# Attention visits of a slot brought together behind the gate, in a fused FFN-attention-FFN block on one core

## The reference, cut to what matters

```
x = x + 0.5 * ffn(layernorm(x))
x = x + attn(layernorm(x))        # 16 heads of 16, 4 KV heads, rope, softmax over 1024 keys
x = x + 0.5 * ffn(layernorm(x))

ffn:  top-8 of 32 experts, cut where the renormalised sum passes 0.8, inner width 96
      out += (silu(x @ Wg.T) * (x @ Wu.T)) @ Wd.T * combine[:, e]     for each expert e
attn: softmax(q @ k.T / 4) @ v, then @ Wo.T
```

## Time and profile before

| what | us |
|---|---|
| median of three runs (2396.12 to 2398.11) | 2397.57 |
| the profiled execution | 2396.93 |
| its span, first to last instruction | 2395.1 |
| TensorE busy | 2280.0 |
| VectorE busy | 1568.7 |
| ScalarE busy | 1235.5 |
| GpSimd busy | 1052.1 |

### The profile page before, as it was taken

One profiled execution on the slowest core, in us unless ns is written; L12 is line 12 of the kernel. 1 busy time (PEld: TensorE's weight loads), 2 busy tenths in 40 slices (PEclk: granted clock), 3 DMA queues, 4 the chain that ended last, 5 costly groups with the idle time before them and its releaser, 6 DMA issues.

```text
span 2395.1 us, 48463 instructions
## 1 busy us (share of the span) xinstructions
PE 2280.0 (95%) x19616; PEld 1517.8 (63%) x19616; DVE 1568.7 (65%) x3106; ACT 1235.5 (52%) x1966; POOL 1052.1 (44%) x864
## 2 busy tenths in 40 slices
PE   0399998999999999999999999999999999999999
PEld 0388885556555555555555555565555655688887
DVE  3855657977777777777777776776776763345443
ACT  1333332256655656656566656666666656633332
POOL 0366664443443443344344433433433433466665
PEclk9999999999999999999999999999999999999999
DMA  4201112101010110111011011100110010010010
GB/s 193 72 19 37 27 41 55 38 18 43 16 35 24 31 38 20 31 26 41 15 33 41 14 34 29 31 19 24 31 30 22 13 29 19 11 37 29 19 38 19
DMA packets 96343, 80.24 MB, mean 33 GB/s; under 512 B 40308, under 2 KB 88692, under 8 KB 95736
## 3 DMA queue, kind: packets, MB, share of 16 engines
q1 hardware_dynamic: 95256, 76.09, 11.3%
q10 hardware_dynamic: 864, 1.05, 0.1%
HBM read 64.25 MB, written 12.85 MB: 32 GB/s over the span
## 4 chain that ended last, share of the span: by engine, by line
PE 91%; DVE 5%; DMA 1%; ACT 1%; issue 1%; SPq 0%; POOL 0%; ACTq 0%; POOLq 0%; DVEq 0%
PE PS L1069 42%; PE PS L1087 21%; PE PS L1099 11%; PE PS L1130 11%; PE PS L1041 2%; DMA arena<-wo 1%; DVE arena L859 1%; PE PS L1111 1%; PE PS L1016 1%; PE PS L1044 1%; PE PS L1171 1%; PE PS L1157 1%; PE PS L1025 0%; DVE arena L836 0%; DVE amax L700 0%
## 5 line engine op out<-in xcount | busy, mean ns | idle before, releaser
L1069 PE MATMUL PS<-XT,WGU 128*128 128x256 f16 x9216 | 1117.3, 274 | 51.2 <-DVE WGU L711 31.7
L1069 PEld LDWEIGHTS PS<-XT,WGU 128*128 128x128 f16 x9216 | 875.2, 98 | 282.7 <-issue 132.6
L520 POOL TENSOR_TENSOR arena<-arena 128x512 f16<-128x512 f32 x384 | 446.8, 1163 | 1198.6 <-ACT arena L596 1198.6
L859 DVE TENSOR_REDUCE arena<-PS 128x1 f32<-128x512 f32 x1024 | 658.2, 685 | 370.6 <-PE PS L1099 368.7
L619 ACT ACTIVATE arena<-PS,fac 128x512 f32<-128x512 f32 x1024 | 646.4, 684 | 236.3 <-PE PS L1111 235.0
L589 ACT ACTIVATE arena<-PS,fac 128x512 f32<-128x512 f32 x384 | 263.9, 687 | 762.1 <-PE PS L1069 762.1
L1087 PE MATMUL PS<-WD,arena 128*128 128x256 f16 x4608 | 568.0, 273 | 1.8 <-POOL arena L520 1.6
L1087 PEld LDWEIGHTS PS<-WD,arena 128*128 128x128 f16 x4608 | 432.4, 98 | 141.3 <-issue 89.8
L515 POOL TENSOR_TENSOR arena<-arena 128x512 f32<-128x512 f32 x384 | 492.0, 1281 | 50.2 <-DVE arena L844 49.0
L836 DVE SCALAR_TENSOR_TENSOR arena<-arena,PS 128x512 f32<-128x512 f32 x384 | 261.2, 680 | 284.1 <-ACT arena L589 283.7
L1099 PE MATMUL PS<-arena 48*128 48x512 f16 x1024 | 312.3, 382 | 7.3 <-DMA arena<-k_scratch 4.6
(11 more groups left out here) (114 smaller groups left out, 856.0 us busy)
## 6 DMA issues: line engine op xcount, KB each, us to landing
arena<-ce_scratch SPq DMA_DIRECT2D x256, 128.0 KB, 3.3
arena<-wgu SPq DMA_DIRECT2D x2, 3072.0 KB, 17.5
arena<-q_scratch SPq DMA_DIRECT2D x96, 64.0 KB, 2.2
arena<-ktab_c SPq DMA_DIRECT2D x16, 256.0 KB, 4.1
q_scratch<-arena SPq DMA_DIRECT2D x32, 128.0 KB, 1.7
out<-X SPq DMA_DIRECT2D x8, 512.0 KB, 3.0
X<-wd SPq DMA_DIRECT2D x1, 3072.0 KB, 28.1
X<-x SPq DMA_DIRECT2D x1, 3072.0 KB, 15.5
```

The lines of the kernel that those rows point to most:

```text
L520: pool.tensor_tensor(hs[1][:, d % HS, :], tw[d % 2], hs[0][:, d % HS, :], ALU.subtract).then_inc(lo_done, 1)
L859: dve.tensor_reduce(mx[:, half * REP * QT + c:half * REP * QT + c + 1], PS[:, B_MAX + half, :], AX_X, ALU.max).then_inc(max_taken, 1)
L1069: ins = pe.matmul(PS[:, b, j * HALF_G:(j + 1) * HALF_G], WGU[w][:, kt, part * CHUNKS + c + j, :], XT[r][:, k % 2, kt, half * HALF_G:(half ...
```

## The change

The visits are arranged anew. TensorE runs visits 0 and 1 directly behind the gate, then up and down, then a second event, then visits 2 and 3, then the first event. VectorE takes both visits' maxima before `gated` and `product`. ScalarE takes visit 0's exponentials before the tanh of the gate, and visit 1's where they were. The table gives four visits to each lead-in slot (ten slots instead of thirteen and a third), and afterwards two, with four in every tenth slot. As the counts are even now, visit 0 is always an even one (scores alone) and visit 1 an odd one, which begins with the value matmuls. Nothing is added or removed: 514 visits with v >= 0, 40 before them, 384 slots. Visits now end in slot 307 instead of 310, and some events move by a few slots.

```diff
-        for pos in range(3 if v < 0 or (d - FIRST) % 5 == 4 else 2):
+        for pos in range(4 if v < 0 or (d - FIRST) % 10 == 9 else 2):
...
 # ScalarE
+                if (d, 0) in VISIT:
+                    visit(VISIT[d, 0])
                 if d + 1 < SLOTS:
                     gate(d + 1)
-                if (d, 0) in VISIT:
-                    visit(VISIT[d, 0])
                 if 0 <= d < SLOTS:
                     high(d)
...
 # VectorE
-                if (d, 0) in VISIT:
-                    visit(VISIT[d, 0])
+                for pos in (0, 1):
+                    if (d, pos) in VISIT:
+                        visit(VISIT[d, pos])
                 if d + 1 < SLOTS:
                     gated(d + 1)
                     product(d + 1)
...
-                if (d, 1) in VISIT:
-                    visit(VISIT[d, 1])
                 if len(EVENTS[d]) > 1:
                     event(d, 1)
...
 # TensorE
                 if d + 1 < SLOTS:
                     gate_or_up(d + 1, 0)
-                if (d, 0) in VISIT:
-                    visit(VISIT[d, 0])
+                for pos in (0, 1):
+                    if (d, pos) in VISIT:
+                        visit(VISIT[d, pos])
                 if d + 1 < SLOTS:
                     gate_or_up(d + 1, 1)
-                if (d, 1) in VISIT:
-                    visit(VISIT[d, 1])
+                if 0 <= d - 1 < SLOTS:
+                    down(d - 1)
                 if len(EVENTS[d]) > 1:
                     event(d, 1)
-                if 0 <= d - 1 < SLOTS:
-                    down(d - 1)
-                if (d, 2) in VISIT:
-                    visit(VISIT[d, 2])
+                for pos in (2, 3):
+                    if (d, pos) in VISIT:
+                        visit(VISIT[d, pos])
                 if EVENTS[d]:
                     event(d, 0)
```

## The result

| | before | changed |
|---|---|---|
| median, us | 2397.63 | 2446.19 |
| runs | 2396.12 to 2398.11 | 2445.95 to 2448.15 |
| span of the profiled execution | 2395.1 | 2444.2 |

The ratio is 1.0205, 95% interval 1.0188 to 1.0223. The forecast was 2419 with a range up to 2438, so the direction was right and the size was less than half of what came: 22 us were forecast and 49 measured. The time is that of the VectorE rival (2445), whose mechanism came in part; that it fits to 1 us is luck. All times are medians of the fast runs; one run of e2_rows, 2941 us at a granted clock of 0.76, is left out.

The account below looks back on a forecast made before the run. TensorE's own order of work was taken to bound the kernel: 2396.9 - 28 (fewer changes) + 23 (second scores) + 16 (lead-in) + 6 (max_rows) + 5 (VectorE's extras) = 2419 us, range 2399 to 2438.

Parts of the forecast that it names:

- VectorE rival: VectorE becomes the bound: norms, joins and output events delay its reductions, 0.2 us on half the pairs; 2445 us, chance 0.15.
- Gain from fewer changes: On TensorE, 11 fewer changes between blocks, scores and values per ten slots, from v = 0: 28 us gained.
- The second scores' wait: Odd visit's scores wait until the even visit's banks are read; next block 0.09 us late in 257 pairs: 23 us lost.
- The lead-in: Paired scores without values between wait for VectorE's reductions; slots of 8.3 us for four visits: 16 us lost.
- max_rows ahead of the product: max_rows of 0.95 us before `gated` delays the product; an event waits 0.7 us, in 8 slots: 6 us lost.
- VectorE's extras: Routing and layernorm pieces after the product make the next slot's reductions late: 5 us lost, bounds 0 and 25.
- The waits of rows 10: TensorE's waits in the body of the visits, a few us in the old profile; left as they are.
- The rival that the values cover the wait: Banks are back when the values end, so the second scores wait for nothing: 2391 us, chance 0.10.

Follow-up runs that it names:

- e2_rows: The changed kernel with max_rows of a slot's first two visits taken behind the product instead of ahead of `gated`: 2437.84 us, ratio 1.0171.
- e5_read: The changed kernel with even visits (v >= 0) reading their second bank over 384 of 512 columns, for maxima and exponentials: 2424.18 us, ratio 1.0113.
- e1_lead: The changed kernel with the lead-in as before, three visits a slot standing apart; new order from v = 0 on: 2431.01 us, ratio 1.0140.
- e13_wait_only: The changed kernel with one addition, GpSimd's weighing waits for VectorE's small operations of the slot: 2436.05 us, ratio 1.0163.
- e7_order: e1_lead with VectorE taking the second visit's maxima behind the product, except in slots of four visits: 2435.34 us, ratio 1.0162.
- e10_wait: e8_sum with GpSimd's weighing waiting for VectorE's small operations, in slots of two visits: 2387.74 us, ratio 0.9959 to the kernel before.
- e8_sum: The changed kernel with e1_lead, e2_rows and ScalarE's repeated wait for values dropped in even visits: 2413.16 us, ratio 1.0064.

## Why the prediction was right or wrong

- *Gain from fewer changes*: right. 257 changes fewer in the trace, the number forecast, at 0.107 us are 28 us; scores directly before values cost the usual 0.11.
- *The second scores' wait*: right. 23 us forecast; 0.087 us x 255 = 22 in the trace, and e5_read took 22 away.
- *The lead-in*: right. Slots of 8.31 us; 16 us forecast, 15 given back by e1_lead.
- *max_rows ahead of the product*: the mechanism was right, the size not. The term was 6 us, from a duration of 0.95 us. Beside GpSimd's `low` it took about 1.6, the event waited 1.44 instead of 0.7, and the gate 0.72 instead of nothing. The blocks of twelve waited 15 us more.
- *VectorE's extras*: this is the step that failed. The term was 5 us, with the durations of the old trace (2.4 us for a routing piece) moved to the new place unchanged. Late maxima cost 22 us, near the term's upper bound of 25, because operations that now stand beside GpSimd's weighing take 1.2 us instead of 0.2. With the two kept apart (e13_wait_only) 9 of the 22 are left, near the term, and 10 of the 49 us of time came back. The waits of rows 10, 7 us, stayed about as large, as the term had it.
- The rival that the values cover the wait fell: the wait of 0.07 to 0.09 stands in every plain pair, and shorter reads (e5_read) took it away.
- The rival "VectorE becomes the bound" gave the time, 2445. Its mechanism, reductions delayed by VectorE's other work, is there, but in 34 visits and not in half of the pairs, and with 15 us of max_rows beside it; that the total agrees is luck. It did not name what made the work longer, GpSimd's operations.
- What was never weighed is what the moved maxima had covered: the two reductions that stood behind the product hid GpSimd's weighing from what follows. I asked what hid each edit on TensorE, not what the moved reductions had hidden on VectorE. e7_order limits this: put back, they hide it again, and nothing is won, for they take as long themselves.

The terms as measured, 28 saved against 22 for the second bank, 17 in the lead-in (21 of waits less 4 for 40 fewer changes), 15 for max_rows, 22 for late maxima and 2 after the visits, make 50 us, against 49 measured. In the forecast the last three were 6, 5 and nothing.

## What to carry to other kernels

When an instruction is moved, ask what it stood between: a duration read from the old trace holds only beside the old neighbours, and here VectorE's small operations on SBUF data grew sixfold beside GpSimd's. Two users of one pair of banks stand side by side without a wait only if what lies between them lasts as long as both reads of the banks. An engine with slack (here GpSimd) can be made to wait so that one without slack is not held up.

## What the runs showed of the hardware

- A small VectorE operation with both inputs in SBUF, begun after a GpSimd operation of 128 x 512, ends about 0.04 us after it: 1.27 us against 0.19 (L784). A `tensor_scalar` with one tensor as input does the same: 1.24 against 0.18 (e2_rows, L869). Reductions from PSUM beside the same operation keep their 0.69 (e10_wait).
- A wait that had long been satisfied still cost ScalarE time, since it stood as an instruction of its own (509 of them at L618 in the changed kernel, 255 in e8_sum): without it the wait for the bank fell by 0.06 us a pair.
